# Second edge layer of a graph network: two groups' products on the two row halves of TensorE, the bias as a 16-bit product of its own

## The reference, cut to what matters

```python
row, col = (edge_index[0], edge_index[1])
h = jnp.concatenate([x[row], edge_attr], axis=1)
h = _lrelu(_bn(h, m1_g1, m1_b1) @ m1_w1 + m1_c1)
h = _lrelu(_bn(h, m1_g2, m1_b2) @ m1_w2 + m1_c2)
h = _bn(h, m1_g3, m1_b3) @ m1_w3 + m1_c3
agg = jax.ops.segment_sum(h, col, num_segments=x.shape[0])
...
```

## Time and profile before

| | |
|---|---|
| median of 3 runs | 25141.51 us (25137.35 to 25158.99) |
| the profiled execution | 25140.86 us, its span 25139.1 us |
| mean granted clock of TensorE over the span | 0.651 of full speed |
| busy share of the span: PE, DVE, POOL, ACT | 59%, 61%, 63%, 21% |
| the second edge layer in the span | about 9286 to 11330 us |

### The profile page before, as it was taken

How to read it: one execution, slowest core, us unless ns; L and a number is a source line. 1 busy time by engine, 2 the same in 40 slices (tenths; PEclk the granted TensorE clock), 3 DMA queues, 4 the chain that set the end, 5 groups by cost and what they waited for, 6 DMA issues and landing times. The chain is left out here.

```text
span 25139.1 us, 445752 instructions
## 1 busy us (share of the span) xinstructions
PE 14765.1 (59%) x102440; PEld 8906.5 (35%) x102441; DVE 15355.5 (61%) x31597; ACT 5180.0 (21%) x13760; POOL 15775.7 (63%) x16798
## 2 busy tenths in 40 slices
PE   7555555576666669995100000000568888888888
PEld 5344444443434348892000000000523333333333
DVE  9766666656565654443111111599578888888888
ACT  4211111111111124441000000000023333333332
POOL 0377777677777764451677777776046666666665
PEclk9655555555555555555555555555579999999999
DMA  2466666633333335540211111122133333433333
GB/s 66 108 173 173 172 173 173 154 69 68 68 68 68 69 77 153 154 128 9 43 40 40 40 40 40 53 72 61 31 100 104 103 103 104 105 103 104 103 104 95
DMA packets 2469135, 2331.19 MB, mean 93 GB/s; under 512 B 1084287, under 2 KB 1990333, under 8 KB 2465922
## 3 DMA queue, kind: packets, MB, share of 16 engines
q1 hardware_dynamic: 1901630, 1900.27, 26.8%
q0 software_dynamic: 412544, 241.53, 6.6%
q10 hardware_dynamic: 153668, 172.93, 2.8%
HBM read 1765.30 MB, written 537.93 MB: 92 GB/s over the span
## 5 line engine op out<-in xcount | busy, mean ns | idle before, releaser
L768 POOL DMA_INDIRECT rows<-split_table,index x3125 | 2995.0, 958 | 1938.5 <-DMA index<-in_src 1007.0
L2255 POOL DMA_INDIRECT rows_x<-x_table,index x3125 | 2972.9, 951 | 1625.9 <-DMA index<-in_src 772.3
L1648 POOL DMA_INDIRECT rows_dram<-rows,place_now x3125 | 3026.2, 968 | 1487.9 <-issue 951.8
L884 POOL DMA_INDIRECT rows<-x_table,index x3125 | 3277.7, 1049 | 1021.1 <-issue 952.0
L1575 DVE TENSOR_REDUCE rows<-banks 128x108 f32<-128x324 f32 x1250 | 490.7, 434 | 3467.4 <-DMA rows_dram<-rows,place_now 3456.0
L1587 PE MATMUL banks<-row_pieces,hot_turned 128*128 x3125 | 393.7, 291 | 3604.0 <-DVE rows L1575 3542.1
L2371 DVE TENSOR_TENSOR second<-banks,h 128x768 f32<-128x768 f32 x2500 | 1944.7, 820 | 896.5 <-PE banks L2520 896.5
L2363 DVE TENSOR_TENSOR first<-banks,h 128x768 f32<-128x768 f32 x2500 | 1934.4, 815 | 155.7 <-issue 120.2
L576 PE MATMUL banks<-counts,low_turned 128*128 128x98 f32 x6250 | 1794.7, 435 | 79.3 <-ACT counts L564 49.5
L576 PEld LDWEIGHTS banks<-counts,low_turned 128*128 128x128 f32 x6250 | 1602.1, 315 | 204.1 <-issue 174.0
L2495 PE MATMUL banks<-u_turned,w_tensor 32*128 32x384 f32 (+1 forms) x10000 | 1529.6, 486 | 145.4 <-DVE second L2371 145.4
(11 more groups left out here) (480 smaller groups left out, 33435.6 us busy)
## 6 DMA issues: line engine op xcount, KB each, us to landing
h<-hidden_dram SPq DMA_DIRECT2D x1250, 320.0 KB
acc_moved<-dst_rows SPq DMA_DIRECT2D x625, 320.0 KB
src_row<-in_src_rows SPq DMA_DIRECT2D x625, 320.0 KB
hot_turned<-turned_dram SPq DMA_DIRECT2D x1250, 160.0 KB, 2.2
hot_dram<-onehot SPq DMA_DIRECT2D x625, 160.0 KB
turned_dram<-hot_turned SPq DMA_DIRECT2D x625, 160.0 KB
a_dram<-a ACTq DMA_DIRECT2D x625, 160.0 KB
a<-a_dram SPq DMA_DIRECT2D x625, 160.0 KB, 2.9
```

The costliest lines, as they stand in the source:

```text
L768: nc.gpsimd.indirect_dma_start(out=m["rows"][j][:, t * SPLIT:(t + 1) * SPLIT], out_offset=None, in_=m["split_table"], in_offset=bass.Indir ...
L884: nc.gpsimd.indirect_dma_start(out=m["rows"][j][:, t * C2:t * C2 + F], out_offset=None, in_=m["x_table"], in_offset=bass.IndirectOffsetOnA ...
L1648: nc.gpsimd.indirect_dma_start(out=m["rows_dram"], out_offset=bass.IndirectOffsetOnAxis(ap=m["place_now"][j][:, t:t + 1], axis=0), in_=m[" ...
L2255: nc.gpsimd.indirect_dma_start(out=m["rows_x"][j][:, t * F:(t + 1) * F], out_offset=None, in_=m["x_table"], in_offset=bass.IndirectOffsetO ...
```

## The change

The products of two groups are issued together. Slots 0 and 1 share one `a1` tile of 128 rows, the even slot on rows 0 to 63, the odd one on rows 64 to 127; slots 2 and 3 share a second tile; slot 4 has the lower half of a third. The scaled weights stand in both halves of `w`, the second by a DMA. TensorE makes the products of slots 0 and 1 in step 2, those of slots 2 and 3 in step 4, that of slot 4 in step 1, the two groups' matmuls alternating; before them it waits for the `a1` of both. The row of ones and the bias row go: the bias is cut into three 16-bit pieces that stand on rows of a 32-row tile, and one matmul for each group (32 rows of 16-bit ones as weights, 320 columns of bias pieces) starts the bank, onto which the products add. SyncE's loads keep their order and their waits.

```diff
+    rows_of = lambda j: slice(j % 2 * H, j % 2 * H + H)
+
     def products_pe(pe, i, j):
-        g = SLOTS * i + j
-        pe.wait_ge(s["a1_in"][j], 16 * (i + 1))
+
+        g = SLOTS * i + j
+        side = [j, j + 1] if j + 1 < SLOTS else [j]
+        for k in side:
+            pe.wait_ge(s["a1_in"][k], 16 * (i + 1))
         if not early(i, g):
-            pe.wait_ge(s["a2_made"], ONE + g - SLOTS + 1)
+            pe.wait_ge(s["a2_made"], ONE + g + len(side) - SLOTS)
         pe.sem_inc(s["going"], 1)
+        for k in side:
+            nc.tensor.matmul(bank(k), m["bias_ones"][:, :], m["bias_rows"][:, :], start=True, stop=False, skip_group_check=True)
         for t in range(T):
-            mm = nc.tensor.matmul(bank(j)[:, t * H:(t + 1) * H], m["a1"][j][0:W, t * P:(t + 1) * P], m["w"][0:W, 0:H], start=True, stop=True)
-        mm.then_inc(s["products"][j], 1)
+            for k in side:
+                mm = nc.tensor.matmul(bank(k)[:, t * H:(t + 1) * H], m["a1"][j // 2][rows_of(k), t * P:(t + 1) * P], m["w"][rows_of(k), 0:H],
+                                      start=False, stop=True, skip_group_check=True)
+                if t == T - 1:
+                    mm.then_inc(s["products"][k], 1)
...
     def step_pe(pe, i, j):
-        if there(i, j, 3):
+        if there(i, j, 3) and at(i, j, 3)[1] % 2 == 0:
             products_pe(pe, *at(i, j, 3))
...
-                sp.dma_start(m["a1"][j][0:H, :], m["a1_dram"][bass.ds(g, 1)].rearrange("g h e -> (g h) e")).then_inc(s["a1_in"][j], 16)
+                sp.dma_start(m["a1"][j // 2][rows_of(j), :], m["a1_dram"][bass.ds(g, 1)].rearrange("g h e -> (g h) e")).then_inc(s["a1_in"][j], 16)
...
-            sp.wait_ge(s["unit_rows"], ONE + 1)
+            sp.wait_ge(s["scaled"], ONE + 1)
+            sp.dma_start(m["w"][H:2 * H, 0:H], m["w"][0:H, 0:H]).then_inc(s["weights"], 16)
...
-            for j in range(SLOTS):
-                link(nc.vector.memset(m["a1"][j][H:H + 1, :], 1.0))
-            nc.vector.nop().then_inc(s["unit_rows"], 1)
...
-            link(nc.vector.tensor_tensor(m["w"][H:H + 1, 0:H], m["sb_m1_c2"][H:H + 1, :], m["ps"][0][H:H + 1, 0:H], ALU.add))
+            left, cut_off, own_row = (m["bias_work"][:, k * H:(k + 1) * H] for k in range(3))
+            piece_now = m["bias_piece"][:, :]
+            bias_rows = m["bias_rows"][:, :].rearrange("p (t h) -> p t h", t=T)
+            link(nc.vector.tensor_tensor(left, m["sb_m1_c2"][0:32, :], m["ps"][0][0:32, 0:H], ALU.add))
+            for k in range(PIECES):
+                link(nc.vector.tensor_copy(piece_now, left))
+                link(nc.vector.tensor_copy(cut_off, piece_now))
+                link(nc.vector.tensor_tensor(left, left, cut_off, ALU.subtract))
+                if k == 0:
+                    link(nc.vector.tensor_scalar(own_row, cut_off, m["ident"][0:32, k:k + 1], None, ALU.mult))
+                else:
+                    link(nc.vector.scalar_tensor_tensor(own_row, cut_off, m["ident"][0:32, k:k + 1], own_row, ALU.mult, ALU.add))
+            link(nc.vector.tensor_copy(bias_rows, rep(own_row, 1, T)))
+            link(nc.vector.memset(m["bias_ones"][:, :], 1.0))
```

More of the change, by code:

```diff
@@ L1205, in _ @@
             link(nc.vector.tensor_scalar(m["w"][0:H, 0:H], m["sb_m1_w2"][:, :], m["a1_stats"][0:H, 2:3], None, ALU.mult))
+            nc.vector.nop().then_inc(s["scaled"], 1)
             nc.vector.tensor_copy(m["wide_shift"][0:H, :], m["a1_stats"][0:H, 3:4].broadcast_to([H, P])).then_inc(s["folded"], 1)
             dve.wait_ge(s["shifted"], ONE + 1)
-            link(nc.vector.tensor_tensor(m["w"][H:H + 1, 0:H], m["sb_m1_c2"][H:H + 1, :], m["ps"][0][H:H + 1, 0:H], ALU.add))
+            left, cut_off, own_row = (m["bias_work"][:, k * H:(k + 1) * H] for k in range(3))
[12 more added lines that the diff above has]
+            link(nc.vector.memset(m["bias_ones"][:, :], 1.0))
             nc.vector.nop().then_inc(s["biased"], 1)
@@ L1220, in _ @@
             pe.wait_ge(s["biased"], ONE + 1)
+            pe.wait_ge(s["weights"], 96)
             in_steps(pe, lambda i, j: step_pe(pe, i, j))
@@ L2873, in build @@
             with ExitStack() as inner:
-                slots("rows", T * H); slots("pieces", T * PIECES * (H + 1), BF16); slots("a1", T * P, parts=H + 1)
+                slots("rows", T * H); slots("pieces", T * PIECES * (H + 1), BF16)
+                m["a1"] = [inner.enter_context(nc.sbuf_tensor(f"a1_{nc.next_id()}", [P, T * P], F32)) for _ in range(3)]
+                sb("bias_work", 3 * H, parts=32, into=inner); sb("bias_piece", H, BF16, parts=32, into=inner)
+                sb("bias_rows", T * H, BF16, parts=32, into=inner); sb("bias_ones", P, BF16, parts=32, into=inner)
                 sb("square_acc", T * H, into=inner); sb("lift2", T * H, into=inner); sb("rest", T * H, into=inner); sb("joined", H + 1, into=inner)
@@ L2878, in build @@
                 stage_edges_second(nc, m, sems(
-                    "second", "step to_root rooted weights folded shifted biased lifted a2_made piece rest second_piece split used squared squares_used square_totals unit_rows "
+                    "second", "step to_root rooted weights folded shifted scaled biased lifted a2_made piece rest second_piece split used squared squares_used square_totals "
                     "windows more_hot summed added gained going all_added halves_in blanked blank_out", "products a1_in hot_in"))
```

## The result

The changed kernel takes **25820.82 us** (median of 4 runs, 25816.85 to 25826.38) against 25140.71 us (median of 4 runs) of the kernel before: a ratio of 1.0269, 95% interval 1.0251 to 1.0287, **slower by 680 us**. The forecast was 25745 us, +604, with a range of 25370 to 26000. The profiled execution took 25822.39 us, its span 25820.6.

What follows compares the result with a forecast made beforehand. TensorE and the load round trip were both taken as close to the bound. Turns of 7.3 (6.9 without a blank) + 4.35 + 5.0 + 4.35 us gave 2614 us against 2010, +604: 25745 us, range 25370 to 26000.

Steps and rivals of the forecast that it cites:

- The wait moves to the odd slot's load: Second edge layer: slot 3's load waits behind slot 2's `used`, putting 5.0 us from sums 2 to the burst.
- The trip from sums 4 to slots 0 and 1: Slot 0's load behind `blank` 7.3 us, slot 1's 6.6 to 7.2; taken as 7.3 with a blank, 6.9 without.
- The burst: A pair on TensorE, wait's end to sums' end: bias 0.54, products 2.28, sums 1.03, row changes 0.5, together 4.35 us.
- 0.5 us together: Three changes of row form in a TensorE burst, drained tails and open loads: 0.5 us, bounds 0 and 1.0.
- The sum: Second edge layer: 98 turns of 21.0 us with a blank, 27 of 20.6 without, 2614 against 2010 us: +604.
- Edits costed at nothing: Five memsets go, some fifteen small bias operations come, weights' copy added; first burst at 9316 to 9319; 1 us added.
- rival 2: TensorE's clock rises to 2.4 GHz in the bursts: -360 us against the forecast, 25380 us; 12%.
- Rival 3: TensorE's row halves don't overlap: each burst 2.28 us longer, +570 us, 26315 us; 8%.
- Rival 1: Loads come in time, TensorE sets the pace: a turn 16.0 us, or 14.2, down to 24905 us; 8%.
- The reading of the kernel before: Second edge layer: 16.08 us a turn against 14.5 for five steps; slot 0's 7.3 us trip behind `blank` already binds.
- five free steps: Second edge layer before: five TensorE steps with sums 2.89 us apart would make a turn of 14.5 us.
- free changes: Lower bound where TensorE's changes of row form cost 0: burst 3.76 us, single 3.49, a turn 14.2 us.

Runs made afterwards that it cites:

- experiments 1 and 2: Changed kernel with both a1 loads of a pair issued ahead of the one-hots: 25351.91 us; then also the store of blank moved behind slots 0 and 1's loads: 25149.82 us.
- experiment 3: Changed kernel with the new products issued one group at a time, no pairs, bias product and row halves kept: 25429.06 us.
- kernel 8: Kernel before, with the store of blank behind slot 0's a1 load and ScalarE's second piece made ahead of the first: 24965.65 us.
- experiment 5: Changed kernel with both groups of a pair on the same lower half of rows, each slot with its own a1 tile: 26366.84 us.
- Rival 1 is kernel 9: Changed kernel with ScalarE's second piece first, each a1 issued as soon as its tile is free, and the store of blank after those loads: 24995.65 us.
- experiment 6: Kernel before with one edit, the store of blank issued behind slot 0's a1 load instead of ahead of it: 25052.93 us.

## Why the prediction was right

Sign and mechanism were forecast, and the time lies inside the range, 76 us above the forecast. By its own steps:

- **The wait moves to the odd slot's load: right.** From sums 2 to the burst 5.0 us were forecast, 4.9 measured (1.9 to the issue, 3.0 from there; the 0.2 us from landing to matmul had been a guess, and against a landing of 2.9 us some 0.1 is left). SyncE still waits for `used`, TensorE's share is 63 to 65% ("near two thirds"), and experiments 1 and 2 take the loss away through SyncE's order alone. The Trainium skill (DMA: Bandwidth & Descriptors, Anatomy of one DMA — SWDGE (gpsimd) path) says that DMA engines don't wait on semaphores, the issuing sequencer does. This trace agrees for SyncE: its wait for `used` (1766 us in all) holds every load behind it, whatever that load needs.
- **The trip from sums 4 to slots 0 and 1: too small.** "That is 6.6 to 7.2 us" for slot 1's load, and 7.3 taken with a blank, 6.9 without; the medians are 8.8 and 7.95. The step let the sums of slot 0 set the pace (done at 10516.16). What paces is VectorE, which handles its steps in order: its reduce for slot 0 comes at 10517.66, 2.92 us after that for slot 4, since the maximum and the squares of another step stand between, and 1.2 us in which the profile shows no wait. So SyncE issues the load 3.4 us after the end of the sums (10516.16 to 10519.54), not 1.9. From there to the burst it takes 4.1 us here, 3.9 in the median of turns with a blank and 3.2 without, not 3.1.
- **The burst: 4.35 us forecast, 3.95 measured** (10510.67 to 10514.62). Bias, products and sums came as forecast. The "0.5 us together" for changes of row form was too much behind a wait: two bias matmuls and a change to 64 rows take 0.62 us where 0.54 of streaming were forecast, and the sums start at 10513.62, as the products end (10513.69). Where nothing waits the changes cost more, 0.36 us a group, because parts that overlapped now start one after the other (experiment 3). The Trainium skill (TensorEngine Tiling (Array Packing), Key Properties) has a change of tiling mode drain TensorE. The runs bear out that it costs, with 0.1 us inside a burst behind a wait and 0.36 us of lost overlap a group without one.
- **The sum.** Two bursts 0.4 us shorter and one trip 1.5 us longer (1.05 without a blank), the other 0.1 shorter, make 0.6 us a turn more with a blank and 0.15 without: 98 x 0.6 + 27 x 0.15 = 63 us, which turns +604 into +667 against the stage's +661. The two misses pointed opposite ways, so the total looks closer than its terms were.
- **Edits costed at nothing: right.** The first matmul of the burst comes at 9317.60 (forecast 9316 to 9319, 9316.21), and it waits for the end of the bias's operations on VectorE, not for the DMA of the weights' copy:

```profile
9317.60 0.69 PE L1070 MATMUL banks<-bias_rows,bias_ones 32*128 32x320 bf16 x2 [4.19 <-DVEq L1231]
```

- **The rivals.** The clock stayed at 0.50 in the changed kernel, and in kernel 8 too, where TensorE is busy throughout: rival 2 did not come. Rival 3 is what experiment 5 builds: forecast +570 on top, measured +546, of which +534 in the stage. Rival 1 is kernel 9: its bounds were 14.2 and 16.0 us a turn, and 14.6 is the answer, which needs three orders changed that the change left alone. The 14.2 takes 3.76 us for a burst with free changes, where the prediction's own terms give 3.85 (4.35 less 0.5); with that the lower bound is 14.5.
- **The reading of the kernel before: half of it.** Of the 1.9 us by which its turns with a blank (16.4 us) exceeded five free steps (14.5), the trip of slot 0's load held 0.8 (experiment 6). Another 1.0 us was ScalarE's order (experiment 8), which the prediction doesn't name. It didn't touch the forecast: in the turn shown above no wait on the path is one for the pieces.

## What to carry to other kernels

Before two units are issued together, look up in the issuing queue what stands ahead of the second unit's load. If it is a wait on the first unit's late consumer, the load comes a step late, and what joining saves on the engine is paid back as waiting. Then price the joined unit whole, with its bias, its lone remainder and the steps that are left empty: here 5.5 us a pair instead of 5.8, and 3.6 for the odd one instead of 2.9, add up to nothing. And look through each in-order engine for an operation that waits for a late producer ahead of one that is ready: exchanging two such lines gave 0.4% here, the new products nothing.

## What had not been expected

- In the kernel before, two exchanged casts on ScalarE were worth 107 us of the stage (kernel 6 to kernel 8), although ScalarE was busy for about half of it. What counts is how late the third piece is, and the page's busy shares don't show it.
- Twenty float32 loads on two halves take 2.21 us where ten on one half take 2.20: each half keeps its own pace of 0.22 us a load, and neither slows the other:

```profile
10511.28 2.21 PEld L1073 LDWEIGHTS banks<-w,a 64*128 64x128 f32 x20 [0.52 <-issue]
...
10516.47 2.20 PEld L1073 LDWEIGHTS banks<-w,a 64*128 64x128 f32 x10 [0.28 <-issue]
```

- Slot 1's `a1`, two loads behind the store of `blank`, lets its burst begin 3.9 us after its issue in the median. In the last turns of the changed kernel, which store no blank, it is 3.2 us, and slot 3's takes 2.9 to 3.0 us in both kinds of turn. So most of the delay comes and goes with the store; whether by its traffic or by its place ahead in the queue no run tells. One turn without a store (the rows that the profile names here were again made long before):

```profile
11615.52 0.48 SPq L1175 DMA_DIRECT2D a<-a_dram  x1
...
11618.76 0.69 PE L1070 MATMUL banks<-bias_rows,bias_ones 32*128 32x320 bf16 x2 [1.88 <-DVE rows L1139]
```
